# The last outputs of an attention layer begun in its score banks, and the next layer's first input and weights prepared inside it

## The reference

```
x = L0_attn_x
x = x + _layernorm(_L0_attn_ref(_layernorm(x, axis=-1), ...), axis=-1)
x = x + _layernorm(_L0_ffn_ref(_layernorm(x, axis=-1), ...), axis=-1)
x = x + _layernorm(_L1_attn_ref(_layernorm(x, axis=-1), ...), axis=-1)
x = x + _layernorm(_L1_ffn_ref(_layernorm(x, axis=-1), ...), axis=-1)

# _L0_attn_ref: 16 heads of 64, causal
dot = jnp.einsum('bqhd,bkhd->bhqk', q, k)
att = jax.nn.softmax(jnp.where(causal, dot, -inf), axis=-1)
out = jnp.einsum('bhqk,bkhd->bqhd', att, v).reshape(bs, n, h * hd)
return out @ w_u + b_u

# _L0_ffn_ref: 8 routed experts (top 2 by a gate), 2 shared ones, each
p1 = x @ w1 + b1;  p2 = x @ w2 + b2
out = (silu(p1) * p2) @ w3 + b3
```

## Time and profile before

| | |
|---|---|
| median of 3 runs | 2395.15 us (2388.61 to 2400.78) |
| the profiled execution | 2398.1 us |
| its span in the trace | 2396.4 us |
| mean granted clock of PE | 0.963 |
| PE busy | 2172.3 us, 91% of the span |
| DVE, ACT, POOL busy | 1444.0, 1206.1, 1042.6 us |
| layer-0 mixture, first up product | starts at 1119.37 us of the span |

### The profile page before, as it was taken

How to read it: one execution, slowest core, us unless ns; L and a number is a source line. 1 busy time by engine, 2 the same in 40 slices (tenths; PEclk the granted TensorE clock), 3 DMA queues, 4 the chain that set the end, 5 groups by cost and what they waited for, 6 DMA issues and landing times. The chain is left out here.

```text
span 2396.4 us, 41419 instructions
## 1 busy us (share of the span) xinstructions
PE 2172.3 (91%) x15940; PEld 1419.7 (59%) x15940; DVE 1444.0 (60%) x3312; ACT 1206.1 (50%) x1788; POOL 1042.6 (44%) x980
## 2 busy tenths in 40 slices
PE   4999999999999999976999999689999998897787
PEld 3555565556555565535888888543444455565667
DVE  4687757776687757753666556546545555556533
ACT  2555535554465535531333323278777866664543
POOL 0777747777677757771323223423323321100001
PEclk8999999999999999997999999789999999899999
DMA  2000000000000000003000000000000000002001
GB/s 76 1 1 1 1 1 1 1 1 1 1 1 1 1 1 1 1 1 74 1 1 1 1 1 1 0 1 1 1 1 1 1 1 1 2 8 71 1 1 36
DMA packets 36328, 18.26 MB, mean 8 GB/s; under 512 B 16667, under 2 KB 33957, under 8 KB 36133
## 3 DMA queue, kind: packets, MB, share of 16 engines
q1 hardware_dynamic: 36132, 15.61, 2.6%
HBM read 13.50 MB, written 2.10 MB: 7 GB/s over the span
## 5 line engine op out<-in xcount | busy, mean ns | idle before, releaser
L343 POOL TENSOR_TENSOR a_first<-a_first,a_ring 128x512 f32<-128x512 f32 (+3 forms) x352 | 556.6, 1581 | 244.0 <-PE a_o_ps L521 206.6
L1843 ACT ACTIVATE g_probsT<-g_s_ps 128x1024 f32<-128x1024 f32 (+2 forms) x448 | 368.9, 869 | 144.1 <-PE g_s_ps L1712 89.6
L625 ACT ACTIVATE a_ring<-a_st 128x768 f32<-128x768 f32 (+1 forms) x256 | 228.6, 918 | 85.7 <-PE a_st L506 83.3
L698 DVE TENSOR_REDUCE a_part_max<-a_mx 128x2 f32<-128x1024 f32 x128 | 156.4, 1222 | 139.7 <-PE a_mx L472 138.2
L721 DVE RECIPROCAL a_row_inv<-a_row_inv 128x256 f32<-128x256 f32 x128 | 218.5, 1731 | 22.0 <-ACT a_row_inv L613 22.0
L521 PE MATMUL a_o_ps<-a_ring,a_v 128*64 128x512 f32 (+3 forms) x1280 | 226.6, 474 | 3.4 <-POOL a_ring L325 3.3
L1113 ACT ACTIVATE m_silu<-m_up,m_b 128x512 f32<-128x512 f32 x160 | 109.6, 688 | 223.8 <-PE m_up L1045 221.0
L1743 PE MATMUL g_o_ps<-g_probsT,g_values 128*32 128x512 f32 (+5 forms) x2688 | 213.6, 430 | 5.2 <-POOL g_probsT L1588 5.1
L1712 PE MATMUL g_s_ps<-g_qT,g_kT 64*128 64x512 f32 (+3 forms) x896 | 173.6, 435 | 27.7 <-ACT g_probsT L1843 22.0
L1588 POOL TENSOR_SCALAR_AFFINE_SELECT g_probsT<-g_probsT 128x512 f32<-128x512 f32 x128 | 88.0, 691 | 252.5 <-ACT g_probsT L1843 252.3
L472 PE MATMUL a_mx<-a_k_hi,a_q_hi 64*128 64x512 f32 (+3 forms) x768 | 146.8, 404 | 24.7 <-DVE a_largest L705 17.5
(11 more groups left out here) (318 smaller groups left out, 4363.6 us busy)
## 6 DMA issues: line engine op xcount, KB each, us to landing
m_w<-in_L_ffn_rw SPq DMA_DIRECT2D x2, 1024.0 KB, 8.5
s_w<-in_L_ffn_w SPq DMA_DIRECT2D x1, 2048.0 KB, 9.8
s_w<-in_L_ffn_w SPq DMA_DIRECT2D x4, 512.0 KB, 10.5
out_x<-x SPq DMA_DIRECT2D x8, 256.0 KB, 2.3
m_w<-in_L_ffn_rw SPq DMA_DIRECT2D x2, 512.0 KB, 5.5
x<-in_L_attn_x SPq DMA_DIRECT2D x1, 512.0 KB, 4.1
a_outT<-in_L_attn_w_q SPq DMA_DIRECT2D x1, 512.0 KB, 4.9
a_outT<-in_L_attn_w_k SPq DMA_DIRECT2D x1, 512.0 KB, 5.8
```

Of the source, the lines that this page charges most:

```text
L343: pool.tensor_tensor(total[:, h, q:q + w], total[:, h, q:q + w], probs_of(n, u)[:, h, off:off + w], ALU.add).then_inc(added, 1)
L625: act.activation(probs_of(n, u)[:, :, 0:w], st_ps[u % 2][:, :, 0:w], ACT.Exp).then_inc(exp_done, 1)
L698: last = dve.tensor_reduce(part_max[:, i, :], mx_ps[:], AX.X, ALU.max)
L1843: act.activation(out, src.rearrange("p k (j n) -> p k j n", j=at_once), ACT.Exp, scale=float(HD) ** -0.5).then_inc(exp_done, 1)
```

## The change

It does five things.

1. PE's output product of batch 3 goes into the score banks `st_ps` instead of `p_ps`, one bank for each quarter, with 128-column weights in place of two halves of 64. It is cut by pair (`output_part`): pairs 0 to 3 stand ahead of the last two weighings, pair 4 ahead of the last row sums, pairs 5 to 7 behind them.
2. The norm and residual of batch 3 leave the attention: they become the pieces `ends` of the mixture's first window (`residual_parts`), and the bias sum is kept in `g.normed`.
3. Batch 0's input for the mixture is normalised, transposed and split in pairs 26 to 29 of the attention, by the code that does it for batches 1 to 3 (as "batch 4").
4. The mixture's gate, `w12` and bias loads are issued by SP in the attention, when the projections have freed the attention's weights, whose space `w12` takes. The first shared expert is split at the end of the attention. The `w3` loads stay in the mixture.
5. An unused mask (`c_mask_kq`), its load and its cast go.

The diff, cut to its core:

```diff
--- before.py
+++ after.py
@@ -177,13 +177,13 @@
     if n == ALL_PAIRS:
-        return [(b, k) for k in range(4)] if t == 4 else []
+        return []
 
-    return [(n // PAIRS + 1, n % PAIRS - 4)] if (n % PAIRS, t) in ((4, 2), (5, 0)) and n // PAIRS + 1 < BATCH else []
+    return [(n // PAIRS + 1, n % PAIRS - 4)] if (n % PAIRS, t) in ((4, 2), (5, 0)) else []
...
+        w_hl = nc.alloc_sbuf_tensor_at("a_w_hl", [P, 6, D * 8], F32R, offset=g.space_at)
+        x_norm = y = g.normed
+        xT_hi, xT_lo = ([g.turned_input[2 * i + part] for i in range(2)] for part in range(2))
...
+            @block.sync
+            def _(sp):
+                sp.wait_ge(qk_done, 4 * ALL_PAIRS)
+                sp.wait_ge(v_done, NB * HALVES)
+                g.mixture.load(nc, sp, g)
...
-                        if (u == 9 and n % PAIRS == 3 and n // PAIRS + 1 < BATCH
+                        if (u == 9 and n % PAIRS == 3
...
-                inverse_root(pool, norm, g.minus_half[:, 0:NB], normed)
...
+                def output_part(t, p):
+                    b = BATCH - 1
+                    if p == 0:
+                        pe.wait_ge(exp_done, ALL_PAIRS * UNITS_A_PAIR - 1 + t // 2)
+                    pe.wait_ge(out_kept, 2 * (b * PAIRS + p) + t // 2 + 1)
+                    for i in range(2):
+                        blk = 2 * t + i
+                        last = pe.matmul(st_ps[t // 2][:, t % 2, i * P:(i + 1) * P],
+                                         outT[:, (b * PAIRS + p) % OUT_SLOTS, blk * P:(blk + 1) * P], w_u[:, p, :],
+                                         start=p == 0 and i == 0, stop=p == PAIRS - 1, skip_group_check=True)
+                    if p == PAIRS - 1:
+                        last.then_inc(y_done, 1)
+
+                def output_parts(pairs):
+                    for t in range(4):
+                        for p in pairs:
+                            output_part(t, p)
...
-                for n in range(-1, ALL_PAIRS + 1):
+                for n in range(-1, ALL_PAIRS):
...
+                output_parts(range(4))
+                add_up_and_weigh(ALL_PAIRS, 0)
+                output_parts([4])
+                add_rows(ALL_PAIRS - 1, 1)
+                output_parts(range(5, PAIRS))
...
-                        if n % PAIRS == 4 and n // PAIRS + 1 < BATCH and t == 0:
+                        if n % PAIRS == 4 and t == 0:
...
-                                normalize_blocks(x_norm, g.x[:, b * NB:(b + 1) * NB, :], x_normed, 2 * b - 1, start)
+                                normalize_blocks(x_norm, g.x[:, b % BATCH * NB:(b % BATCH + 1) * NB, :], x_normed, 2 * b - 1, start)
+
+                g.mixture.split_high(act, E_ROUTED)
...
-                    dve.tensor_tensor(y[:, 2 * t:2 * t + 2, :], p_ps[:, 0:2 * P].rearrange("p (t n) -> p t n", t=2),
+                    src = p_ps[:, 0:2 * P] if b + 1 < BATCH else st_ps[t // 2][:, t % 2, 0:2 * P]
+                    dve.tensor_tensor(y[:, 2 * t:2 * t + 2, :], src.rearrange("p (t n) -> p t n", t=2),
...
+                        if b == BATCH:
+                            dve.wait_ge(residual_done, 2)
...
-                def finished_last(b, count):
-
-                    y_of = lambda blk: y[:, blk, :]
-                    x_all = g.x[:, b * NB:(b + 1) * NB, :]
-                    dve.wait_ge(y_kept, 4 * b + 4)
-                    layernorm(dve, chain, y_of, y_of, norm, count)
-                    chain.did(dve.tensor_tensor(x_all, x_all, y[:], ALU.add))
-                    chain.settle()
...
-                normalizing = {b: normalized(b) for b in range(1, BATCH)}
+                normalizing = {b: normalized(b) for b in range(1, BATCH + 1)}
...
-                finished_last(BATCH - 1, 2 * BATCH - 1)
+                g.mixture.split_low(dve, E_ROUTED)
+                for part in range(4):
+                    add_bias(BATCH - 1, part)
...
+class MixtureStart:
...
+    def load(self, nc, sp, g):
+        for letter, e0, n, w_sem in (("s", E_ROUTED, E_SHARED, self.sw_loaded), ("r", 0, E_ROUTED, self.rw_loaded)):
+            for j in range(2):
+                sp.dma_start(self.w12[:, e0:e0 + n, j, :], g.inputs[f"L0_ffn_{letter}w{j + 1}"]
+                             .rearrange("e p n -> p e n")).then_inc(w_sem, 16)
+        sp.dma_start(self.gate_w[:], g.inputs["L0_ffn_gate_w"]).then_inc(self.small_loaded, 16)
+        sp.dma_start(self.gate_b[:], g.inputs["L0_ffn_gate_b"].partition_broadcast(P)).then_inc(self.small_loaded, 16)
+        sp.dma_start(self.iota[:], g.inputs["c_iota"].partition_broadcast(P)).then_inc(self.small_loaded, 16)
+        with nc.allow_non_contiguous_dma(reason="biases, one value per partition"):
+            for letter, e0, n, b_sem in (("s", E_ROUTED, E_SHARED, self.sb_loaded), ("r", 0, E_ROUTED, self.rb_loaded)):
+                for j in range(2):
+                    src = g.inputs[f"L0_ffn_{letter}b{j + 1}"].rearrange("e (h p) -> p (e h)", p=P)
+                    sp.dma_start(self.b12[:, j, e0:e0 + n, :].rearrange("p e h -> p (e h)"), src).then_inc(b_sem, 16)
+
+    def split_high(self, act, e):
+        act.wait_ge(self.sw_loaded, 2 * 16)
+        act.activation(self.high[:], self.w12[:, e], ACT.Copy).then_inc(self.first_high, 1)
+
+    def split_low(self, dve, e):
+        dve.wait_ge(self.first_high, 1)
+        dve.tensor_tensor(self.low[:], self.w12[:, e], self.high[:].bitcast(F32), ALU.subtract).then_inc(self.first_low, 1)
...
+        xT_hi = [g.turned_input[0]] + [sb(f"xT_hi{b}", [P, SEQ], F32R) for b in range(1, BATCH)]
+        xT_lo = [g.turned_input[1]] + [sb(f"xT_lo{b}", [P, SEQ], F32R) for b in range(1, BATCH)]
...
+                for letter, e0, n, w3_sem in (("s", E_ROUTED, E_SHARED, sw3_loaded), ("r", 0, E_ROUTED, rw3_loaded)):
...
-                inverse_root(pool, norm, g.minus_half[:, 0:NB], 0)
-                pool.wait_ge(rw_loaded, 2 * 16)
+                pool.wait_ge(start.rw_loaded, 2 * 16)
...
-                    if s < M_UNITS and (i == RESIDUAL_ROOT_AT and s >= M_WINDOW
-                                        or i == NEXT_ROOT_AT):
+                    if s < M_UNITS and i in (RESIDUAL_ROOT_AT, NEXT_ROOT_AT):
...
-                    if place_of_unit(u) == 0 and h == 0:
-                        pe.wait_ge(xT_lo_done, b * 2 + half_of_unit(u) + 1)
-                    if b == 0 and half_of_unit(u) == 0 and h == 0:
-                        pe.wait_ge(w_split, place_of_unit(u) + 1)
-                    cols = cols_of(b, half_of_unit(u))
+                    if b and place_of_unit(u) == 0 and h == 0:
+                        pe.wait_ge(xT_lo_done, b * 2 + half_of_unit(u) - 1)
+                    if b == 0 and place_of_unit(u) and half_of_unit(u) == 0 and h == 0:
+                        pe.wait_ge(w_split, place_of_unit(u))
+                    cols = cols_of(half_of_unit(u))
...
-                turn_input(0, 0)
...
-                    if u == 0:
-                        turn_input(0, 1)
...
-                act.wait_ge(sw_loaded, 2 * 16)
-                for e in range(E_ROUTED, EXPERTS):
-                    act.activation(w_hi[:, e], w12[:, e], ACT.Copy).then_inc(shared_hi, 1)
-                keep_high(0, 0)
+                for e in range(E_ROUTED + 1, EXPERTS):
+                    act.activation(high_of(e), w12[:, e], ACT.Copy).then_inc(shared_hi, 1)
...
-                    if u == 0:
-                        keep_high(0, 1)
...
-                first = norm_of(0)
...
-                for part_of_norm in first[0:5]:
-                    part_of_norm()
-                split_low(0)
-                for part_of_norm in first[5:7]:
-                    part_of_norm()
-                low_input(0, 0)
...
-                        ends = residual(b - 1) if b else []
+                        ends = residual(b - 1) if b else residual_parts(BATCH - 1, g.normed[:])
...
-        "c_mask_kq": np.where(i[:, None] > i[None, :], -1e30, 0.0).astype(np.float32),
...
+        g.turned_input = [nc.alloc_sbuf_tensor_at(f"turned_input{i}", [P, SEQ], F32R, offset=hidden_at + i * SEQ * 4)
+                          for i in range(4)]
...
-                sp.dma_start(staged[0][:, 0:P], g.inputs["c_mask_kq"]).then_inc(const_loaded, 16)
-                sp.dma_start(staged[1][:], g.inputs["c_mask_window"]).then_inc(const_loaded, 16)
+                sp.dma_start(staged[:], g.inputs["c_mask_window"]).then_inc(const_loaded, 16)
```

More of the change, by code:

```diff
@@ L730, in normalized @@
                 def normalized(b):
-                    parts = layernorm_parts(dve, chain, lambda blk: g.x[:, b * NB + blk, :], None, norm, None, -0.5,
+                    parts = layernorm_parts(dve, chain, lambda blk: g.x[:, b % BATCH * NB + blk, :], None, norm, None, -0.5,
                                             True)[:7]
@@ L779, in pieces_of_phase @@
                         pieces += finishing[b - 1][start:stop]
-                    if n > 0 and b + 1 < BATCH and t in NORMALIZING.get(pair, {}):
```

(30 more changed lines are left out.)

93 lines of the change are left out of this document (36 added, 57 removed).

## The result

The changed kernel takes 2356.26 us (median of 4 runs, 2354.27 to 2360.87) against 2393.89 (4 runs) for the kernel before: ratio 0.9844, 95% interval 0.9813 to 0.9876. Measured again, with 6 runs against 11, it takes 2358.34 against 2388.04, ratio 0.9862 (0.9838 to 0.9885). So 30 to 38 us are gone, where 34.7 were forecast and 2360.5 was the time given. Between executions of one program the time varies by some 10 us (2349.01 to 2362.21 in the six).

A forecast was written before the change was run, and what follows sets the result against it. PE bounds the mixture, but the border before it is a relay where nothing overlaps. Terms -37.3 + 2.2 + 3.5 - 2.6 + 0 - 0.5 = -34.7 take 2398.1 to 2363.4; less 2.95, 2360.5 us, range 2350 to 2376.

The forecast's parts named there:

- the likeliest case: The forecast's own sum of its terms for the whole kernel: 2360.5 us, chance 0.48.
- (a): Attention's end, last scaling to the mixture's first up product: 41.06 us falls to 3.8, gain 37.3.
- (b): Attention's tail: output products put ahead of the row sums delay them on in-order PE, loss 2.2 us.
- (c): Late attention pairs: making batch 0's input costs time where PE is the bound, +3.5 us, bounds 0 and 3.5.
- (d): Mixture's start, first 24 up products and logits: 12.90 us falls to 10.3, gain 2.6, bounds 0.7 and 4.5.
- (e): First mixture window: batch 3's residual norm moves in there without holding up PE, 0 us.
- (f): Program's start: one load and a small cast less, gain 0.5 us, bounds 0 and 0.6.
- The median: Whole kernel: 2.95 us taken off the profiled time, as that execution stood above the median of its runs.
- full clock throughout: Rival: PE's clock never falls between 1063 us and the mixture, (d) gives 4.5 us, total 2358.6; chance 0.20.
- The early parts at half clock: Rival: the 80 records ahead of the row sums run at half clock, 8 us more there, total 2372; chance 0.14.
- Less idle, more throttling: Rival: less rest brings ten more half-clock spells in the busy layers behind, 17 us lost, total 2377.5; chance 0.09.
- held up the first window: Rival: DVE's residual pieces stop PE in units 4 to 10, 2410 us at 7 us each; chance 0.04.

The follow-up runs named there:

- best: Changed kernel with logits spread over unit 0, the last outputs reordered and the first expert split before the last inversions: 2341.04 us, ratio 0.9789.

## Why the prediction was right

The time lay in its range, and the likeliest case in its place: 2356.3 and 2358.3 measured, 2360.5 given. The mechanism held as well: the signs named came, with the first up product at 1086.74 (about 1087 given), 64 records in 7.41 us at full clock, and the row sums 2.9 us later within the last pairs. Over the stretch that the sum is about, from pair 27 to the third layer, 34.2 us were forecast without the program's start; the two profiles show 32.8 and 37.1.

- **(a) From scaling to first up product**, 41.06 us to 3.8: measured 4.65, and 5.0 in the repeat. The step held; barrier and wake-up took 0.97 us together instead of 1.25. The last 16 records took 3.18 us, not 1.95, as the clock fell to 0.50 behind the 1.99 us wait. That wait does not settle it: with spread logits the same 1.99 us stood there, the clock stayed up and they took 2.05.
- **(b) Row sums held up**, +2.2: measured +2.05, by the forecast's own parts (64 records 7.41 us against 7.46, the full clock for the row sums 1.08). What the sum left out is small: the first expert's split does not lie free under the relay but lengthens the scaling, +0.27. The early parts themselves are worth 4 us in the trace, by the run that put them all behind.
- **(c) Batch 0's input**, +3.5: measured +3.74. Batch 3's lighter pairs absorb nothing, as PE is their bound.
- **(d) The mixture's start**, -2.6 with bounds 0.7 and 4.5: measured -0.42 in the first profile, -3.05 in the second, -4.50 with spread logits, and +0.2 with the tail reordered. One number could not be right here. The small bound was too hopeful by 0.3. The reason given, "PE comes out of two waits", named only one place where the clock falls: in the first profile it fell again at about 1093, in the middle of the stretch, behind the start of the logits. But as the reordered run shows, it can fall there with spread logits too.
- **(e) The residual norm among the units**, 0: the run with and without it gives 0.12 us. The Trainium skill ("SBUF — State Buffer", "Who interferes with whom") calls the port pair that DVE and POOL share an exclusive lock; the traces agree, with 1.52 us for a scaling beside a split and 1.26 without. Nothing comes of it where PE is the bound. Ahead of the barrier it does reach the relay, with 0.27 us, and there the sum had not looked for it. The first window did get about 1 us longer, by its up products and not by these pieces.
- **(f) The program's start**, -0.5: can't be seen, since the stretch ahead of pair 27 varies by 6.6 us between executions.
- **The median**, taken as 2.95 us below the profiled execution: a fair guess at a spread that is 10 us wide. The remaining 2 to 4 us by which the measured time was lower are inside it. That the total came this close is partly luck: (d) and the up products gave some 3 us less than forecast in the first profile, and the clock gave 3.1 more in the later windows, which no term was about.

Of the rivals, full clock throughout came true in one run alone, with spread logits and the old order of the tail. "The early parts at half clock" did not occur: 64 records took 7.41 us. "Less idle, more throttling" had the sign wrong, the mixture's clock being 0.99 instead of 0.98 in this execution. No wait held up the first window.

Two executions of one program differ by 8.3 us in the part behind the mixture. The first profile alone would have credited the change with 43.8 us, and nothing in that profile says otherwise; the repeat did.

## What to carry to other kernels

A border between two stages is a relay of short steps on engines that all wait; cost it from the release that nobody can move (here POOL's last addition) and count what must stand behind it, product by product. Work that fills a wait on an in-order engine should end when the wait ends: three pairs ahead of the row sums fitted, five held them up by nearly 3 us, and none left 4 us unused. Where a busy engine's clock dips at regular places, look at what ran just ahead of each dip. And where runs vary by 10 us, compare one stretch of the traces, not the totals, and profile the same program twice.

## What the runs showed of the hardware

TensorE's clock fell to 1.2 GHz behind a run of 24 products of 128 by 8, although PE was busy without a gap in the record: 6.60 us at clock 1.00 with that run in it, then 3.40 us at 0.50. Such a fall came with 14 of 21 such runs. With six such products between groups of wide ones the clock stayed at 1.00 in all nine windows behind the first, in both kernels. A short spell there costs 1.6 to 1.7 us, a long one 3.3; on the kernel before, 8 us went by the medians and 6.8 by the trace. Whether it is their 8 columns or their number in a row was not separated. The Trainium skill ("TensorE: Matmul & The Clock Gate", "What's actually happening") has the clock set by how busy PE has been. The trace can't say whether that covers this case: from 1191.79 to 1194.50 PE is busy 2.71 us and its weight loads 2.70, so the busy share does not tell multiplying from loading.

In `best`, the run with the tail reordered, the weight split on DVE took 1.07 us instead of 0.63, and POOL's diagonal cut 0.86 instead of 0.41:

```profile
1062.48 2.35 POOL L347 TENSOR_TENSOR a_first<-a_first,a_ring 128x1024 f32<-128x1024 f32 x1 [0.17 <-POOL a_first L347]
1064.31 1.07 DVE L904 TENSOR_TENSOR m_first_low<-m_w,m_first_high 128x512 fp32r<-128x512 f32 x1 [3.85 <-ACT m_first_high L900]
1064.79 0.86 POOL L329 TENSOR_SCALAR_AFFINE_SELECT a_ring<-a_ring 128x256 f32<-128x256 f32 x1
```

Read in order, these are two waits and not one mutual slowing. The split began at 1064.31 beside an addition that POOL had been at since 1062.48 and that ended at 1064.83; its usual 0.63 us from there gives 1065.46, and it ended at 1065.38. The cut began at 1064.79, beside the split; its usual 0.41 from the split's end gives 1065.79, and it ended at 1065.65. So each was held up by what the other engine had begun before it, to within 0.14 us.
